# Four edits around the edges of a two-layer kernel: bonus copies, centred weights, first round, last round

## The reference, cut to what matters

```
x  = L0_attn_x                                   # (2, 1024, 256)
xn = layernorm(x)
s  = attn0(xn)                                   # RWKV6: 4 heads of 64
g  = silu(ffn0(xn))                              # 1024 hidden units, 2 of 4 kept
x  = x + s * g
xn = layernorm(x)
s  = attn1(xn)                                   # state-space, 8 heads of 64
g  = silu(ffn1(xn))                              # 1024 hidden units
x  = x + s * g

# in attn0, per token t and head:
r, k, v = xr @ W_r.T, xk @ W_k.T, xv @ W_v.T
g  = silu(xg @ W_g.T)
w  = time_decay + tanh(xw @ w1) @ w2 ; d_t = exp(-exp(w))
y  = r_t . (S + u * k_t (x) v_t) ;  S = d_t * S + k_t (x) v_t     # u is the bonus
yn = (y - mean(y)) * rsqrt(var(y) + eps)         # over the 64 channels of a head
out = (yn * gamma + beta) * g @ W_o.T
```

## Time and profile before

| what | value |
|---|---|
| median of 3 runs | 749.4 us (748.67 to 750.21) |
| the profiled execution's own time | 750.87 us |
| its span (first to last instruction) | 749.1 us |
| PE busy | 723.5 us (97%), 6906 matmul records |
| DVE busy | 530.1 us (71%) |
| ACT busy | 316.9 us (42%) |
| POOL busy | 76.2 us (10%) |
| DMA queue of SP | 54.76 MB, 29.7% of 16 engines |
| granted TensorE clock, mean | 0.999 |

### The profile page before, as it was taken

How to read it: one execution, slowest core, us unless ns; L and a number is a source line. 1 busy time by engine, 2 the same in 40 slices (tenths; PEclk the granted TensorE clock), 3 DMA queues, 4 the chain that set the end, 5 groups by cost and what they waited for, 6 DMA issues and landing times.

```text
span 749.1 us, 17781 instructions
## 1 busy us (share of the span) xinstructions
PE 723.5 (97%) x6906; PEld 590.5 (79%) x6906; DVE 530.1 (71%) x1200; ACT 316.9 (42%) x652; POOL 76.2 (10%) x85
## 2 busy tenths in 40 slices
PE   5899999999999999999989999999999999999897
PEld 3777778877888778887778867888778878888686
DVE  3996789836897568956789467984679837896143
ACT  1322583226821466214841058411683236811570
POOL 6201101101011011000110001100101101010020
PEclk9999999999999999999999999999999999999999
DMA  8910451035400363013620145201540036400360
GB/s 277 359 45 0 125 81 27 1 86 142 73 2 11 105 128 58 2 29 101 121 51 2 29 142 86 45 1 44 166 81 10 1 85 142 72 2 14 114 113 16
DMA packets 121597, 55.93 MB, mean 75 GB/s; under 512 B 104305, under 2 KB 113585, under 8 KB 119857
## 3 DMA queue, kind: packets, MB, share of 16 engines
q1 hardware_dynamic: 121520, 54.76, 29.7%
HBM read 42.35 MB, written 12.40 MB: 73 GB/s over the span
## 4 chain that ended last, share of the span: by engine, by line
PE 91%; DVE 5%; issue 2%; ACT 0%; DMA 0%; POOL 0%; DVEq 0%; SPq 0%; ACTq 0%; POOLq 0%
PE psum L1378 71%; PE psum L1480 3%; PE psum L1587 2%; PE psum L1572 2%; PE psum L1451 1%; PE psum L1598 1%; PE psum L1625 1%; PE psum L1793 1%; PE psum L1493 1%; PE psum L1406 1%; PE psum L1440 1%; PE psum L1463 1%; PE psum L1735 1%; PE psum L1672 1%; PE psum L1516 1%
## 5 line engine op out<-in xcount | busy, mean ns | idle before, releaser
L582 ACT ACTIVATE BC<-psum 64x256 f32<-64x256 f32 x128 | 80.9, 632 | 3.5 <-PE psum L1378 1.8
L1378 PE MATMUL psum<-xnT,sb_f_gate 128*128 128x256 f32 x248 | 62.2, 394 | 0.8 <-ACT xnT L595 0.8
L1378 PE MATMUL psum<-xn1T,sb_n_gate 128*128 128x256 f32 x256 | 61.4, 383 | 0.0
L1378 PE MATMUL psum<-xn1T,sb_n_up 128*128 128x256 f32 x256 | 60.5, 379 | 0.0
L1378 PE MATMUL psum<-xnT,sb_f_up 128*128 128x256 f32 x240 | 59.0, 388 | 0.0
L1378 PEld LDWEIGHTS psum<-xn1T,sb_n_up 128*128 128x128 f32 x256 | 48.6, 190 | 6.6
L1378 PEld LDWEIGHTS psum<-xnT,sb_f_gate 128*128 128x128 f32 x248 | 46.7, 194 | 8.5 <-ACT xnT L595 1.2
L1378 PEld LDWEIGHTS psum<-xn1T,sb_n_gate 128*128 128x128 f32 x256 | 47.4, 190 | 6.5
L1378 PEld LDWEIGHTS psum<-xnT,sb_f_up 128*128 128x128 f32 x240 | 43.6, 189 | 7.5 <-DVE S L1075 1.7
L1378 PE MATMUL psum<-sb_f_down,hid 128*128 128x256 f32 x224 | 49.5, 379 | 0.0
L1378 PE MATMUL psum<-sb_n_down,hidB 128*128 128x256 f32 x224 | 49.5, 379 | 0.0
(11 more groups left out here) (216 smaller groups left out, 1515.8 us busy)
## 6 DMA issues: line engine op xcount, KB each, us to landing
cs_row<-cs_dram SPq DMA_DIRECT2D x8, 1024.0 KB, 4.9
x_dram<-gate SPq DMA_DIRECT2D x8, 512.0 KB, 2.8
cs_half<-cs_dram SPq DMA_DIRECT2D x16, 256.0 KB, 5.7
hidB<-x_dram SPq DMA_DIRECT2D x8, 512.0 KB, 5.8
b_dram<-B_turned SPq DMA_DIRECT2D x32, 128.0 KB, 3.2
hidB<-b_dram SPq DMA_DIRECT2D x8, 512.0 KB, 4.3
X<-in_x SPq DMA_DIRECT2D x9, 256.0 KB, 3.5
XT<-in_x_turned SPq DMA_DIRECT2D x8, 256.0 KB, 3.4
```

Source lines behind the costliest of these rows:

```text
L582: ins = a_.activation(cols[:, par, 2 * pair:2 * pair + 2, :], src[64 * par:64 * par + 64, :, s, :], ACT.Identity)
L1378: ins = t_.matmul(ps(t, name)[first_row:first_row + rows, col:col + n], w, x, start=(k == 0), stop=(k == len(ws) - 1))
```

## The change

Four parts. (1) ACT makes the two kinds of columns of rU first and the plain rT last; PE's `first_levels` waits for rU alone, and DVE's first `level_step` for the bank of r. (2) Since y is linear in v, the mean over a head's 64 channels is taken out of the columns of the weights of v, once, in the first round on DVE (`weights_centred`); the sum, scaling and subtraction on y fall away in each tile, and `centred` becomes `gathered`. (3) The first round is in another order: PE takes `rank_mix` after half of p0g and `mixes` before p0u; weights are loaded in another order and in smaller parts; DVE's `next_normed` moves behind `variances`; unused matmuls are 1 and 1 where they were 7. (4) In the last round ACT's `x1_kept` stands between the two `x_copy`; the last output is made, and stored, in two halves of 128x256.

```diff
 # SP: loads
-            load(["w_dec1", "w_rkvgo"], "proj")
-            load_twice("w_dec2", "proj")
-            ffn_units(2 * P, HID, "ffn0_rest")
+            sp_.dma_start(values_in, A["w_rkvgo"][:, 4 * C:6 * C]).then_inc(loads["values"], 16)
+            load(["w_dec1"], "decay")
+            load_twice("w_dec2", "decay")
+            ffn_units(2 * P, 4 * P, "ffn0_pair1")
+            for n in (slice(0, 4 * C), slice(6 * C, 10 * C)):
+                sp_.dma_start(W["w_rkvgo"][:, n], A["w_rkvgo"][:, n]).then_inc(loads["proj"], 16)
+            ffn_units(4 * P, HID, "ffn0_rest")
...
 # SP: one()
+                    if b.last:
+                        for q in range(NQ):
+                            wait(out_ready, b.count(1, 2) + q)
+                            sp_.dma_start(A["out"][bass.ds(b.at() * T + q * P, P), :], thFB[:, q * C:(q + 1) * C]).then_inc(
+                                out_stored, 16)
+                        return
...
 # ACT: receptances()
-                    a_.activation(flat(rT), ps(a, "r")[:, :], ACT.Identity)
                     a_.activation(rU[:, :, 64:96], by_64[:, :, 1:64:2], ACT.Identity)
...
-                    free(ins, a, "r")
+                    ins.then_inc(rU_ready, 1)
+                    free(a_.activation(flat(rT), ps(a, "r")[:, :], ACT.Identity), a, "r")
...
 # ACT: squares()
-                    act.wait_ge(yc_ready, a.count(1, 1))
-                    a_.activation(flat(ysq), flat(yc), ACT.Square).then_inc(ysq_ready, 1)
+                    wait_freed(act, a, "Y1")
+                    a_.activation(flat(ysq), flat(y), ACT.Square).then_inc(ysq_ready, 1)
...
 # ACT: last round
-                    x1_kept()
                     steps_copied()
                     softplus()
                     x_copy(b, 0)
+                    x1_kept()
                     x_copy(b, 1)
...
 # DVE: level_step(), n == 0
+                    wait_freed(dve, t, "r")
...
 # DVE
+                def weights_centred():
+                    dve.wait_ge(loads["values"], 16)
+                    w = values_in.rearrange("p (n d) -> p n d", d=HD)
+                    did(d.tensor_reduce(gsum[:, :], w, AX.X, ALU.add))
+                    after()
+                    did(d.tensor_scalar(gsum[:, :], gsum[:, :], 1.0 / HD, None, ALU.mult))
+                    after()
+                    d.tensor_tensor(w, w, gsum[:, :].unsqueeze(2).to_broadcast([P, CH * HEADS, HD]),
+                                    ALU.subtract).then_inc(values_centred, 1)
...
-                def centred():
+                def gathered():
...
                     free(d.tensor_tensor(y5[64:P], y5[64:P], Y5[64:P], ALU.add), a, "Y1")
-                    after()
-                    wait_freed(dve, a, "Y1")
-                    did(d.tensor_reduce(gsum[:, :], y3, AX.X, ALU.add))
-                    after()
-                    did(d.tensor_scalar(gsum[:, :], gsum[:, :], 1.0 / HD, None, ALU.mult))
-                    after()
-                    d.tensor_tensor(yc3, y3, gsum[:, :].unsqueeze(2).to_broadcast([P, NQ * HEADS, HD]),
-                                    ALU.subtract).then_inc(yc_ready, 1)
...
 # DVE: result()
+                    if b.last:
+                        for q in range(NQ):
+                            half, name = slice(q * C, (q + 1) * C), f"s1{'ab'[q]}"
+                            wait_filled(dve, b, name)
+                            free(d.tensor_tensor(thFB[:, half], thFB[:, half], ps(b, name)[:, 0:C], ALU.mult), b, name)
+                            wait_freed(dve, b, name)
+                            d.scalar_tensor_tensor(out=thFB[:, half], in0=thFB[:, half], scalar=0.125, in1=x1_prev[:, q, :],
+                                                   op0=ALU.mult, op1=ALU.add).then_inc(out_ready, 1)
+                        return
...
 # DVE: first round
                     state_kept()
+                    weights_centred()
...
                     states_0()
-                    next_normed()
                     sparse_compare(a, 1, 1)
                     sparse_compare(a, 1, 2)
                     sparse_count()
-                    centred()
+                    gathered()
                     sparse_select(1)
                     variances()
-                    gate_0()
+                    next_normed()
                     out_normed()
+                    gate_0()
                     out_gated()
...
 # PE: first_levels()
-                    wait_freed(pe, a, "r")
+                    pe.sem_inc(passed, 1)
+                    pe.wait_ge(rU_ready, a.count(1, 1))
...
 # PE: first round
-                    project_p(a, 0, "g")
+                    half_p(a, 0, "g", 0)
                     rank_mix()
-                    project_p(a, 0, "u")
+                    half_p(a, 0, "g", 1)
                     mixes()
+                    project_p(a, 0, "u")
...
+                    kept_at_work("p2u", 1)
                     level(a, 1)
...
-                    kept_at_work("yT", 7)
+                    kept_at_work("yT", 1)
...
 # PE: last round
-                    out_1()
+                    wait_freed(pe, b, "ys0")
+                    wait_freed(pe, b, "ys1")
+                    for q in range(NQ):
+                        project(b, f"s1{'ab'[q]}", [(0, P, [gate[:, m, q * P:(q + 1) * P] for m in range(SH // 2)],
+                                                    [W["w_sout"][:, m * C:(m + 1) * C] for m in range(SH // 2)])])
```

37 lines of the change are left out of this document (23 added, 14 removed).

## The result

| what | before | after |
|---|---|---|
| median | 749.4 us (748.65 to 751.72, 5 runs) | 743.76 us (742.86 to 745.26, 5 runs) |
| the profiled execution's own time | 750.87 us | 742.86 us |
| its span | 749.1 us | 741.1 us |
| PE busy | 723.5 us | 720.3 us |
| DVE busy | 530.1 us | 517.5 us |

The ratio is 0.9922, with a 95% interval of 0.9902 to 0.9942: 5.6 us faster, where 7.5 were forecast. The forecast of 741.9 us was 1.9 us too low; the time lies above the forecast's own 740.5 to 743.2, and within the 740.2 to 744.6 that took in rivals 1 and 2. It lies nearest to rival 1, whose time was 743.5. One execution of all (761.84 us in experiment 6, mean granted clock 0.950) is over 1.5% slower than the fastest of its kernel, and the ratios leave it out.

What follows compares the result with a forecast made beforehand. PE bounds the loop, busy 99.71 of 100 us; slack lies in the first and last rounds and behind the last matmul. Terms -1.6 - 1.9 - 2.3 - 1.0 - 0.7 = -7.5 us from 749.4 give 741.9; range 740.5 to 743.2.

Steps and rivals of the forecast that it cites:

- rivals 1 and 2: Gap before L1493 stays (0.14), or the first round's start or end gains less as another chain takes over (0.20); to 744.6.
- rival 1: Loop: the gap before L1493 is PE's sequencer's own, not ACT's, and stays; 743.5 us, up to 743.8; chance 0.14.
- part 1: Loop: rU ready about 0.5 us sooner closes PE's gap before L1493, -1.6 us over six rounds.
- part 2: Loop: centring gone saves some 11 us of DVE, but PE waits for nothing there: worth 0.
- 3a: First round's start: mixes ahead of p0u remove PE's 1.72 idle before decay_in; everything behind moves by -1.9 us.
- 3b: First round's end, DVE's chain: centring gone and next_normed moved under POOL's 1.6; out_normed and what follows -2.3 us.
- 4a: Last round: steps copied first, PE gains 1.55 us, gives 0.55 back at states through the displaced copy: -1.0.
- 4b: Behind the last matmul: half-size DVE instructions -0.5, store of half the bytes -0.2; together -0.7 us.
- Rival 3: First round's end: fewer unused matmuls leave PE idle, TensorE falls to its lower level and stays, slower; chance 0.04.

Runs made afterwards that it cites:

- experiment 6: Changed kernel with next_normed back ahead of the comparisons in the first round, and gate_0 back ahead of out_normed: 745.98 us, ratio 0.9929.
- experiment 7: Changed kernel with ACT's x1_kept put first again, ahead of the copy of the steps, in the last round: 744.48 us, ratio 0.9943.
- experiment 5: Study of the granted clock: changed kernel without unused matmuls in the first round, 746.40 us; with seven ahead of the selection again, 744.33 us.
- experiment 2: Changed kernel with D0 and D1 moved to the banks behind mix_g0 and mix_g1, away from r's bank: 742.28 us, ratio 0.9889.
- experiment 1: Changed kernel with rT made ahead of rU again and PE waiting for the freed bank: 745.05 us, ratio 0.9931.
- experiment 8: Changed kernel with SP storing the sums ahead of Xnat in the last round: 743.55 us; with D0 and D1 in other banks too: 740.81 us.
- the kernel before with POOL's wait: Kernel before, with POOL's product cs_half made to wait until DVE has scaled B: 749.58 us, ratio 0.9992.
- 5b: Changed kernel with seven unused matmuls ahead of the selection again instead of one: 744.33 us, ratio 0.9944.
- experiment 4: Changed kernel with DVE's scaling of B made to start together with POOL's product: 765.77 us; POOL waiting for DVE instead: 744.84 us, on the kernel before 749.58 us.
- experiment 3: Changed kernel with D0 and D1 in other banks and rT made ahead of rU again: 742.90 us, ratio 0.9907.

## Why the prediction was right, and where not

The mechanism of four of five terms was as told; one term, part 1, brought less than half of its size, or nothing. The found numbers are differences between traces of single executions, except where an experiment is named.

| term | forecast | found | by |
|---|---|---|---|
| part 1, loop | -1.6 | 0 to -0.7 | six gaps left; experiments 1 to 3 |
| part 2, loop | 0 | 0 | PE 99.71 and 99.70 of 100 |
| 3a, start | -1.9 | -2.0 in the pair, -1.2 to -1.4 at the same rise of the clock | first level's products 33.67 to 31.66; see below |
| 3b, end | -2.3 | -2.0 | updates of S to `out_normed`: 11.63 to 9.67 |
| 4a | -1.0 | -1.0 | experiment 7 |
| 4b | -0.7 | -1.0 | 7.83 to 6.80 |
| lowered clock | not in the sum | +0.7, an estimate | experiment 5 |

*Part 1* failed at the sentence "With rT last, rU is ready about 0.5 us sooner, so PE would be free to start at 453.6". rU was ready sooner and PE was not free. In front of the new wait stood the one for D0's bank, whose last reader had just become rT. The forecast read that the 0.34 held a late release, which was right. It was released by the freed bank, though, and not by a finished rU. Nothing in the trace before tells the two apart, since one copy did both: the last copy out of r freed the bank and finished rU. The table of turns tells them apart, and so would the waits that stand in front of the product in PE's list. Rival 1, that the gap is PE's sequencer's own, had the right time; it is right for the 0.13 to 0.24 that the loop adds, and by itself that would not have made the gap (experiment 2).

*Part 3a*: the idle before `decay_in` has gone and `mixes` come first, as told, but the size is partly luck: the changed kernel's trace has the earliest rise of the clock (12.1 us), 1.3 us ahead of that of the kernel before (13.4). Two kernels with the new order and a rise at 13.3 show the rest. In experiment 1 `mixes` start at 14.73 and `decay_in` at 17.85, 1.8 and 1.6 us ahead of the kernel before, and the updates of S at 48.63, only 1.2 ahead of 49.86; in experiment 8, with rT last, they start at 48.45, 1.4 ahead. The forecast had DVE's chain move by as much as PE's. In the changed kernel's trace there is also a loss: DVE's last mixed input took 1.11 us instead of 0.69 while POOL made its masks.

```profile
22.05 1.63 POOL L535 CAST same<-ident 64x512 int8<-64x512 f32 x2
22.09 1.11 DVE L914 TENSOR_TENSOR mixed_v<-mixed_v,xnT 128x512 f32<-128x512 f32 x1
```

*Part 3b* lacks 0.3. The step is "`next_normed` (1.5 us) fits under POOL's 1.6": it fits, and makes POOL's 1.6 a 2.0 (experiment 6).

*Part 4a* was right in size, yet the pair of traces shows only 0.3 at `states` (30.17 to 29.90). In the kernel before with POOL's wait, whose last round is in the old order too, it is 31.15. The old trace had the faster DMAs: from the issue of Xnat's store to that of B's load it took 17.20, against 18.02 there, 17.80 in experiment 7 and 17.75 in the changed kernel. A pair of traces alone would have called this term missed. The half microsecond that the displaced copy was to give back came too: PE's wait before `states` is 1.27 with part 4a and 0.70 without (experiment 7). *Part 4b*: both stores land in 1.7 us, as a store of 32 KB did, so the store is worth 0.5 and not 0.2.

*Rival 3* does not hold as it was told: the granted clock does not fall and stay, and in the traces of kernels with one unused matmul for seven the falls lie ahead of that place. What does happen in many executions is a fall for 3.4 us, at about 1.7 us each. The share of executions with a mean clock of 0.998 or less is 16 of 49 before and 46 of 63 after, 0.4 more, and 0.4 of 1.7 gives +0.7. This is an estimate: that a fall costs as much in the kernel before is not shown. The forecast had set this rival against gaps of 1.7 that did no harm in one trace. One trace is one draw. Which edit makes the falls more frequent stays open; it is not the unused matmuls ahead of the selection (5b). Nor is it that PE's idle time now lies closer together. The four us in which PE is busy least ahead of the first place of the falls, before and then after:

```profile
31.00:35.00 4.00, 2.68 (x45) 2.06 (x42) 3.05 (x8) 1.07 (x2) 0.31 (x1) 1.00 0.98 396
28.95:32.95 4.00, 2.63 (x43) 1.98 (x42) 3.05 (x8) 0.71 (x2) 0.36 (x1) 1.00 1.03 421
```

Ahead of the second place, up to `chunk_states`, it is 2.18 in both. Neither trace has a fall in the first round.

The found column adds up to -6.0 + 0.7 = -5.3 with 3a as in the pair of traces and nothing for part 1. With 3a at the same rise of the clock it is -4.5 to -4.7, and part 1 can take 0.7 off either. The medians are 5.6 apart, with an interval of 4.3 to 7.3, so the account closes to about a microsecond and no better. The two profiled executions are 8.0 apart, and the 743.4 forecast for the profiled one was missed by only 0.5. That is luck: 2.6 of the 8.0 is the one collision of before, and 0.6 to 0.8 the early rise of the clock.

## What to carry to other kernels

Before an operand is made ready earlier for a consumer, list every wait in front of that consumer, the one for its output's bank included; where one instruction ends two of them, the trace can't tell which mattered, and moving a copy may only move the release. Time under a POOL instruction that reads SBUF is no free cover for DVE work with two inputs in SBUF: here it made POOL's part longer (1.64 to 2.02), or DVE's (0.62 to 2.77). And where one execution differs from the next by a microsecond in one place, price an edit by undoing it on the same side, with distances inside a round, not by the two traces of before and after.

## What was not expected of the hardware

- One DVE product of 0.62 us takes 2.77 when POOL has begun a product of 2.4 us. POOL's power on 128x8 took 2.02 beside DVE instructions with both inputs in SBUF, and 1.64 beside one that reads an input from PSUM.
- The granted clock fell to 1.2 GHz for 3.4 us (6.8 in two traces) behind stretches in which PE was idle a third to half of the time, in some executions of a kernel and not in others, and even in some rounds of one execution and not in others (experiment 4). The profile of the kernel before shows no fall ahead of its last two microseconds.
- The first rise to 2.4 GHz came between 12.1 and 15.5 us of the span in 14 traces, and what came behind it moved by up to 1.6 us.
- A store of 128 KB landed in 1.7 us, like one of 32 KB; one of 256 KB took 2.2.
- In the rounds of the hardware loop PE started 0.34 us behind the end of the copy that it waited for (0.24 in experiment 3), and in the same code written out, in round 7, 0.10 to 0.21 behind it.
